# A four-stage vision block on one core: the weighting of a gathered row as one VectorE multiply or as four

## The chip, the cores and the metric

The kernel runs on one core of one Trainium2 chip. The metric is the device time of one execution in microseconds. Three runs of the kernel before took 13376.52, 13376.6 and 13379.08 us; the median is 13376.6 us.

## The reference

The input `x` is (4, 128, 128, 64) in float32. Four layers follow each other, each behind a residual or a normalisation: a 3x3 convolution with a 1x1 (L0), a deformable convolution (L1), a focal modulation with depthwise convolutions of 3, 5 and 7 taps (L2), and a triangle multiplication (L3). The change touches L1 alone. For each pixel, each of 2 channel groups and each of 9 taps, a position is worked out from learnt offsets, and 32 channels are sampled there bilinearly:

```python
out = wa[..., None] * gather(y0i, x0i) + wb[..., None] * gather(y1i, x0i) \
    + wc[..., None] * gather(y0i, x1i) + wd[..., None] * gather(y1i, x1i)
...
s = sampled.reshape(B, H, W, Kin)
s = _conv_same(s, dw_w[g], dw_b[g], groups=Kin)
s = _conv_same(s, pw_w[g], pw_b[g])
```

So 18 samples (2 groups by 9 taps) of four corners and 32 channels are wanted for every pixel.

## The kernel before

**The table.** Per image the kernel writes a table to device memory in which one entry holds the whole 2x2 patch of one group at one position: four corners of 32 channels, 128 floats (512 bytes). One indirect DMA, issued by GpSimd at L451, fetches one such entry for each of 128 pixels: an image row of 128 pixels lies across the 128 partitions, and `gat[r]` is [128, 18, 128]. A row of pixels thus takes 18 gathers. There are 4 images of 128 rows: 512 rows and 9216 gathers.

**The step.** Four rows (r = 0 to 3) make a step; each r has its own buffer `gat[r]`, its own indices `idx[:, r]` and its own semaphore `landed[r]`. GpSimd does nothing but this in the main part. Before the 18 gathers of row r it waits for `idx_given` (the indices of this row were copied) and for `summed` (the row that was in this buffer one step ago has been used up):

```python
pool.wait_ge(idx_given, v + 1)
pool.wait_ge(summed, v + 1)
```

**The row on VectorE.** `row()` waits for `landed[r]` and then issues, in this order: a copy of the next step's indices (`give_indices`, L1382), the multiply of all of `gat[r]` by the corner weights `wt` (L1406, 2304 elements per partition, both inputs in SBUF), a copy of the next weights (`give_weights`, L1385), the add of the right half of each entry to the left (L1411, 1152 elements, both inputs in SBUF), and the add of the two that remain into `srow` (L1418, 576 elements, both in SBUF). TensorE then turns `srow` (L1078, L1079), ScalarE copies it (L862, L863), and TensorE multiplies it with the folded depthwise and pointwise weights (L1085).

**What lies beside it.** `drive()` and `weave()` lay the stages of the other layers over the steps: while the gathers of image b run, VectorE, ScalarE and TensorE also work on the convolution, table and offsets of later images or on the modulation and triangle stages of the image before. Between two phases of `row()` (its `yield`s) their instructions stand on VectorE, as the `scalar_tensor_tensor` of L1291 and L1299, which read one input in PSUM, `bn_stats` at L1144, or the add at L1343 (`tt(res[u], lin[u], xt(...), ALU.add)`), which has both inputs in SBUF and 512 elements and is issued twice in a row. Before the first gather stands a prologue for image 0, and behind the last gather the remaining stages of image 3 run without any gather.

Of the kernel before, what the change touches and what calls it, by code (L numbers as in the profile page):

```python
# [25 lines left out]
ALU = mybir.AluOpType  # L26
# [5 lines left out]
P = 128  # L32
# [8 lines left out]
G, CG = 2, 32  # L41
GK = G * K9
# [128 lines left out]
def build(nc, x, mats, vecs, conv_kt, conv_w, off_w, dw_w, pw_w, dw_b, gate_w, base_loc, base_idx, taps,  # L171
          out):
    ctx = ExitStack()
    with ctx:
        def sb(name, shape, dt=F32):
            return ctx.enter_context(nc.sbuf_tensor(name, shape, dt))
# [4 lines left out]
        def sems(*names):  # L181
            return tuple(ctx.enter_context(nc.semaphore(n)) for n in names)
# [51 lines left out]
        wt = sb("wt", [P, ROWS, GK, 4])  # L234
# [61 lines left out]
        with nc.Block() as block:  # L296
# [64 lines left out]
        weighted, summed, turned, st_ready, rows_used, pair_done, pair_added, xr_in, x2_out = sems(  # L361
            "weighted", "summed", "turned", "st_ready", "rows_used", "pair_done", "pair_added", "xr_in", "x2_out")
# [68 lines left out]
        with nc.Block() as block:  # L431
# [705 lines left out]
            def _(dve):  # L1137
# [3 lines left out]
                stt_, tt, ts = nc.vector.scalar_tensor_tensor, nc.vector.tensor_tensor, nc.vector.tensor_scalar  # L1141
# [239 lines left out]
                def give_indices(v, r):  # L1381
                    nc.vector.tensor_copy(idx[:, r, :], idxn[:, r, :]).then_inc(idx_given, 1)  # L1382

                def give_weights(v, r):
                    nc.vector.tensor_copy(wt[:, r, :, :], wtn[:, r, :, :]).then_inc(wt_given, 1)  # L1385
# [10 lines left out]
                def row(n, r, give):  # L1396

                    v = n * ROWS + r
                    yield 3 * r
                    dve.wait_ge(landed[r], 16 * GK * (n + 1))  # L1400
                    if give:
                        give_indices(v, r)
                    dve.wait_ge(wt_given, v + 1)
                    g4 = gat[r][:].rearrange("p k (q c) -> p k q c", q=4)
                    wb = wt[:, r, :, :].unsqueeze(3).to_broadcast([P, GK, 4, CG])
                    tt(g4, g4, wb, ALU.mult).then_inc(weighted, 1)  # L1406
                    yield 3 * r + 1
                    dve.wait_ge(weighted, 2 * v + 1)
                    if give:
                        give_weights(v, r)  # L1410
                    tt(gat[r][:, :, 0:2 * CG], gat[r][:, :, 0:2 * CG], gat[r][:, :, 2 * CG:], ALU.add)\  # L1411
                        .then_inc(weighted, 1)
                    yield 3 * r + 2
                    dve.wait_ge(weighted, 2 * v + 2)
                    dve.wait_ge(turned, v + 1)
                    dst = srow[r % 2][:].rearrange("p (k g c) -> p g k c", g=G, c=CG)
                    src = gat[r][:].rearrange("p (g k) e -> p g k e", g=G)
                    tt(dst, src[:, :, :, 0:CG], src[:, :, :, CG:2 * CG], ALU.add).then_inc(summed, 1)  # L1418
# [12 lines left out]
                def step(n, b, i):  # L1431
                    last = isinstance(n, int) and n == STEPS - 1
                    yield 0
                    if isinstance(i, int) and i == PER - 1 and not last:
                        next_image(b + 1)
                    if not last:
                        indices(n + 1)
                    for r in range(ROWS):
                        yield from row(n, r, not last)
                        if r % 2 == 1:  # L1440
                            finish(n, r // 2)
                    if last:

                        dve.wait_ge(pair_done, 2 * STEPS + 1)
                        dve.wait_ge(x2_out, 16 * STEPS)
                        dve.wait_ge(xr_in, 16 * STEPS + 16)
                        stt_(xs[:, 0, :], acc[1][:, 0:W], b1, xr[:, 0, :], ALU.add, ALU.add).then_inc(pair_added, 1)
# [134 lines left out]
```

## Time and profile before

| | |
|---|---|
| median of three runs | 13376.6 us |
| profiled execution, first to last instruction | 13375.1 us |
| GpSimd (POOL) busy | 9661.0 us, 72% |
| TensorE matmul (PE) busy | 8114.2 us, 61% |
| VectorE (DVE) busy | 4255.4 us, 32% |
| ScalarE (ACT) busy | 1677.8 us, 13% |
| first gather starts, last gather starts | 242.7 us, 12686.7 us |

The time of the profiled execution is known by its span; it lies 1.5 us below the median of the runs. GpSimd's busy time counts the gathers' issue (the making of their descriptors), not the transfers, and the 0.30 us in front of each gather, in which its sequencer works for the next one, are not counted as busy. Busy shares are of the whole span, with the prologue and the end, in which GpSimd is idle.

### The profile page before, as it was taken

How to read it: one execution, taken by the hardware profiler on the slowest of the kernel's cores; microseconds unless marked ns; L12 is line 12 of the kernel's file. 1: busy time of each engine (PE TensorE's matmuls, PEld its weight loads, DVE VectorE, ACT ScalarE, POOL GpSimd, SP SyncE). 2: the span in 40 equal slices, each digit the busy share in tenths (PEclk: the TensorE clock that was granted, in tenths of full speed). 3: DMA queues.
4: the chain of work that ended last, by engine and by line, in shares of the span. 5: the costliest groups of instructions: out<-in, count | busy, mean ns of one | idle time of the engine just before them, and what ended most of it. 6: DMA issues, size and time to landing. Idle time of an engine off the chain costs nothing.

```text
span 13375.1 us, 136898 instructions
## 1 busy us (share of the span) xinstructions
PE 8114.2 (61%) x46082; PEld 6501.7 (49%) x46082; DVE 4255.4 (32%) x6850; ACT 1677.8 (13%) x3045; POOL 9661.0 (72%) x9269
## 2 busy tenths in 40 slices
PE   5666667666467765554457665654456675655487
PEld 3444445444456644444346654444446654444473
DVE  3233333333233332232233333232233333233233
ACT  1001101011010112110010011210000011210015
POOL 2777777777777777777777777777777777777700
PEclk7787778777678777776678777777678787777688
DMA  3333434334233422332233422332224422332164
GB/s 103 92 84 102 115 83 120 103 91 117 66 118 132 136 61 72 102 92 57 59 98 132 158 62 66 93 102 66 53 74 134 159 86 59 85 109 76 50 239 127
DMA packets 1033598, 1315.00 MB, mean 98 GB/s; under 512 B 186529, under 2 KB 831329, under 8 KB 1015969
## 3 DMA queue, kind: packets, MB, share of 16 engines
q0 software_dynamic: 294912, 604.57, 17.3%
q1 hardware_dynamic: 661664, 657.15, 15.0%
q10 hardware_dynamic: 76800, 50.34, 1.2%
q8 instruction: 138, 2.26, 0.1%
q14 instruction: 84, 0.68, 0.0%
HBM read 1082.07 MB, written 292.16 MB: 103 GB/s over the span
## 4 chain that ended last, share of the span: by engine, by line
POOL 71%; issue 22%; PE 3%; DMA 1%; DVE 1%; ACT 0%; SPq 0%; POOLq 0%; DVEq 0%; ACTq 0%; PEld 0%; PEldq 0%
POOL gat L451 71%; PE stage L982 2%; PE stage L885 1%; DMA table<-room 0%; PE acc L885 0%; DMA room<-b_d 0%; POOLq L449 0%; PE pt L885 0%; PE ptl L885 0%; PE stage L937 0%; POOLq L447 0%; POOLq L457 0%; DMA room<-x 0%; ACT room L776 0%; PE acc L1085 0%
## 5 line engine op out<-in xcount | busy, mean ns | idle before, releaser
L451 POOL DMA_INDIRECT gat<-table,idx x9216 | 9636.5, 1046 | 3010.1 <-issue 2804.4
L1085 PE MATMUL acc<-stt,wk 128*128 128x128 f32 (+1 forms) x30600 | 4502.0, 311 | 315.6 <-ACT stt L863 315.6
L1085 PEld LDWEIGHTS acc<-stt,wk 128*128 128x128 f32 (+1 forms) x30600 | 4259.1, 221 | 744.1 <-ACT stt L863 445.2
L1078 PE MATMUL pt<-mat,srow 128*128 128x128 f32 x2048 | 524.3, 405 | 3993.4 <-DVE srow L1418 3992.8
L1078 PEld LDWEIGHTS pt<-mat,srow 128*128 128x128 f32 x2048 | 342.4, 203 | 4193.4 <-DVE srow L1418 4167.2
L1382 DVE COPY idx<-idxn 128x18 uint32<-128x18 uint32 x512 | 98.1, 192 | 7115.7 <-DMA gat<-table,idx 7107.6
L885 PE MATMUL stage<-room,mat 128*128 128x512 f32 (+1 forms) x1696 | 1037.3, 745 | 574.2 <-DVE room L1291 124.4
L1406 DVE TENSOR_TENSOR gat<-gat,wt 128x2304 f32<-128x2304 f32 x512 | 1309.0, 2557 | 76.5 <-DMA gat<-table,idx 75.8
L862 ACT ACTIVATE stt<-pt 128x512 f32<-128x512 f32 x512 | 305.6, 597 | 7527.7 <-PE ptl L1079 7399.5
L982 PE MATMUL stage<-room 128*128 128x128 f32 x7680 | 892.4, 278 | 20.8 <-DMA room<-toep 18.7
L982 PEld LDWEIGHTS stage<-room 128*128 128x128 f32 x7680 | 877.2, 194 | 31.0 <-issue 22.3
L885 PEld LDWEIGHTS stage<-room,mat 128*128 128x128 f32 x1696 | 377.4, 247 | 1004.2 <-issue 468.3
L1411 DVE TENSOR_TENSOR gat<-gat 128x1152 f32<-128x1152 f32 x512 | 691.9, 1351 | 0.1
L1418 DVE TENSOR_TENSOR srow<-gat 128x576 f32<-128x576 f32 x512 | 388.5, 759 | 14.8
L937 PE MATMUL stage<-room,offw 128*72 (+1 forms) x768 | 369.6, 633 | 14.6 <-SPq L405 12.9
L913 PE MATMUL stage<-room,cw 128*128 (+1 forms) x768 | 347.4, 607 | 16.5 <-ACTq L405 14.3
L1361 DVE TENSOR_TENSOR loc<-off,base 128x144 f32<-128x144 f32 x128 | 39.3, 307 | 802.8 <-DMA off<-offs 802.8
L760 ACT ACTIVATE room<-stage 128x512 f32<-128x512 f32 x192 | 115.1, 599 | 1032.4 <-PE stage L982 1032.1
L913 PEld LDWEIGHTS stage<-room,cw 128*128 128x128 f32 x768 | 144.5, 193 | 189.9 <-issue 185.7
L937 PEld LDWEIGHTS stage<-room,offw 128*72 128x72 f32 x768 | 112.6, 154 | 222.9 <-issue 209.7
L1079 PE MATMUL ptl<-mat,srow 128*64 128x128 f32 x512 | 201.1, 393 | 0.0
L691 ACT ACTIVATE room<-room,gn 128x512 f32 x256 | 192.3, 805 | 37.6 <-PEq L405 35.9
(180 smaller groups left out, 4031.3 us busy)
## 6 DMA issues: line engine op xcount, KB each, us to landing
gat<-table,idx POOLq DMA_INDIRECT x9216
room<-toep SPq DMA_DIRECT2D x64, 1792.0 KB, 18.4
room<-toep SPq DMA_DIRECT2D x64, 1280.0 KB, 11.3
table<-room SPq DMA_DIRECT2D x128, 512.0 KB
room<-toep SPq DMA_DIRECT2D x64, 768.0 KB, 5.0
toep<-in_taps SPq DMA_DIRECT2D x128, 224.0 KB
toep<-in_taps SPq DMA_DIRECT2D x128, 160.0 KB
room<-in_x SPq DMA_DIRECT2D x4, 4096.0 KB, 15.2
```

The source lines that it names most:

```text
L451: nc.gpsimd.indirect_dma_start(gat[r][:, k, :], None, table[b][0:NENT * ENTRY].rearrange("(n e) -> n e", e=ENTRY), bass.IndirectOffsetOnAx ...
L862: nc.scalar.activation(stt[r % 2][:, 0:4, 1:W + 1], pt[:], ACT.Copy)
L885: return nc.tensor.matmul(dst, w, r, start=True, stop=True)
L913: ins = nc.tensor.matmul(PB[u][:], cw0[:, 2 * k:2 * k + 2, :].rearrange("p a c -> p (a c)"), window(k // 3, k % 3, t), start=(k == 0), sto ...
L937: ins = nc.tensor.matmul(PB[0][0:2 * NOFF, :], offw[:, k, :], window(k // 3, k % 3, 2 * i + u), start=(k == 0), stop=(k == 5))
L982: ins = nc.tensor.matmul(PB[2 * u + l % 2][:, c * W:(c + 1) * W], band[l][u][:, c * k + dx, :], cin[l][u][:, c, at:at + W], start=(dx == 0 ...
L1078: nc.tensor.transpose(pt[:, m, :], srow[r % 2][:, m * P:(m + 1) * P], M["ident"])
L1079: nc.tensor.transpose(ptl[:, r % 2, :], srow[r % 2][:, 4 * P:KC], M["ident"]).then_inc(turned, 1)
L1085: ins = nc.tensor.matmul(acc[a][:, 0:W], wk[0:kk, m, dx, block_at * C:block_at * C + P], stt[s][0:kk, m, dx:dx + W], start=start and m == ...
L1406: tt(g4, g4, wb, ALU.mult).then_inc(weighted, 1)
L1411: tt(gat[r][:, :, 0:2 * CG], gat[r][:, :, 0:2 * CG], gat[r][:, :, 2 * CG:], ALU.add)\
L1418: tt(dst, src[:, :, :, 0:CG], src[:, :, :, CG:2 * CG], ALU.add).then_inc(summed, 1)
```

## The change

In `row()` the one multiply becomes four, one for each corner q of the 2x2 patch. Each multiplies the 32 channels of that corner in all 18 entries (18 x 32 = 576 elements per partition, in chunks of 32 with a step of 128) by the weight of that corner. They work in place on separate parts of `gat[r]`; the first waits for `wt_given` as the one multiply did, and none of the others waits for anything. All four count up `weighted`, so the two waits behind them count in fives.

```diff
@@ -1402,16 +1402,17 @@
                         give_indices(v, r)
                     dve.wait_ge(wt_given, v + 1)
                     g4 = gat[r][:].rearrange("p k (q c) -> p k q c", q=4)
-                    wb = wt[:, r, :, :].unsqueeze(3).to_broadcast([P, GK, 4, CG])
-                    tt(g4, g4, wb, ALU.mult).then_inc(weighted, 1)
+                    for q in range(4):
+                        wb = wt[:, r, :, q:q + 1].to_broadcast([P, GK, CG])
+                        tt(g4[:, :, q, :], g4[:, :, q, :], wb, ALU.mult).then_inc(weighted, 1)
                     yield 3 * r + 1
-                    dve.wait_ge(weighted, 2 * v + 1)
+                    dve.wait_ge(weighted, 5 * v + 4)
                     if give:
                         give_weights(v, r)
                     tt(gat[r][:, :, 0:2 * CG], gat[r][:, :, 0:2 * CG], gat[r][:, :, 2 * CG:], ALU.add)\
                         .then_inc(weighted, 1)
                     yield 3 * r + 2
-                    dve.wait_ge(weighted, 2 * v + 2)
+                    dve.wait_ge(weighted, 5 * v + 5)
                     dve.wait_ge(turned, v + 1)
                     dst = srow[r % 2][:].rearrange("p (k g c) -> p g k c", g=G, c=CG)
                     src = gat[r][:].rearrange("p (g k) e -> p g k e", g=G)
```

On VectorE the row r = 1 of the first step reads so in the program before (the words in brackets are the semaphores that an instruction waits for):

```order
L1382 COPY idx<-idxn 128x18 [waits landed1]
L1406 TENSOR_TENSOR gat<-gat,wt 128x2304 [waits wt_given]
L1385 COPY wt<-wtn 128x72 [waits weighted]
L1411 TENSOR_TENSOR gat<-gat 128x18x64
L1418 TENSOR_TENSOR srow<-gat 128x2x9x32 [waits turned,weighted]
```

and so in the changed one, where the lines behind the multiply have moved on by one:

```order
L1382 COPY idx<-idxn 128x18 [waits landed1]
L1407 TENSOR_TENSOR gat<-gat,wt 128x18x32 [waits wt_given]
L1407 TENSOR_TENSOR gat<-gat,wt 128x18x32 x3
L1385 COPY wt<-wtn 128x72 [waits weighted]
L1412 TENSOR_TENSOR gat<-gat 128x18x64
L1419 TENSOR_TENSOR srow<-gat 128x2x9x32 [waits turned,weighted]
```

Nothing else moves: the three other multiplies stand directly behind the first, and no instruction of another stage comes between them. The other engines' programs are the same.

## Rows read from the trace of the kernel before

**Rows 1.** The page: busy time and shares, and the busy tenths in 40 slices.
```profile
PE 8114.2 (61%) x46082; PEld 6501.7 (49%) x46082; DVE 4255.4 (32%) x6850; ACT 1677.8 (13%) x3045; POOL 9661.0 (72%) x9269
...
DVE  3233333333233332232233333232233333233233
...
POOL 2777777777777777777777777777777777777700
```

**Rows 2.** The page: the chain of waits that ended last, by engine and line.
```profile
POOL 71%; issue 22%; PE 3%; DMA 1%; DVE 1%; ACT 0%; SPq 0%; POOLq 0%; DVEq 0%; ACTq 0%; PEld 0%; PEldq 0%
```

**Rows 3.** Costliest groups: busy, mean ns of one | idle just before, what ended it.
```profile
L451 POOL DMA_INDIRECT gat<-table,idx x9216 | 9636.5, 1046 | 3010.1 <-issue 2804.4
...
L1382 DVE COPY idx<-idxn 128x18 uint32<-128x18 uint32 x512 | 98.1, 192 | 7115.7 <-DMA gat<-table,idx 7107.6
```

**Rows 4.** The gather's line: ns min/median/max, first and last start, its waits.
```profile
L451 POOL DMA_INDIRECT gat<-table,idx x9216: 940/944/3314, 242.7 to 12686.7; - x197
...
  issue: 2804.4, 9202
  DVE idx L1382: 202.1, 2
  DVE srow L1418: 3.7, 12
```

**Rows 5.** Timeline: start us, us, engine line op, [idle before <-releaser]; one row of pixels.
```profile
5020.16 0.94 POOL L451 DMA_INDIRECT gat<-table,idx  x1 [0.30 <-issue]
5021.41 0.94 POOL L451 DMA_INDIRECT gat<-table,idx  x1 [0.30 <-issue]
5021.52 0.18 DVE L1382 COPY idx<-idxn 128x18 uint32<-128x18 uint32 x1 [16.67 <-DMA gat<-table,idx]
5021.61 2.56 DVE L1406 TENSOR_TENSOR gat<-gat,wt 128x2304 f32<-128x2304 f32 x1
5022.66 2.33 POOL L451 DMA_INDIRECT gat<-table,idx  x1 [0.30 <-issue]
5024.09 1.40 DVE L1291 SCALAR_TENSOR_TENSOR room<-stage,vec,room 128x512 f32<-128x512 f32 x2
...
5025.29 0.94 POOL L451 DMA_INDIRECT gat<-table,idx  x1 [0.30 <-issue]
...
5025.51 1.35 DVE L1411 TENSOR_TENSOR gat<-gat 128x1152 f32<-128x1152 f32 x1
...
5026.54 1.14 POOL L451 DMA_INDIRECT gat<-table,idx  x1 [0.30 <-issue]
...
5026.90 0.76 DVE L1418 TENSOR_TENSOR srow<-gat 128x576 f32<-128x576 f32 x1
```

**Rows 6.** Timeline: the multiply of the next step, met earlier by a gather.
```profile
5053.65 2.55 DVE L1406 TENSOR_TENSOR gat<-gat,wt 128x2304 f32<-128x2304 f32 x1
5054.19 2.82 POOL L451 DMA_INDIRECT gat<-table,idx  x1 [0.31 <-issue]
...
5056.42 1.35 DVE L1411 TENSOR_TENSOR gat<-gat 128x1152 f32<-128x1152 f32 x1
5057.32 1.27 POOL L451 DMA_INDIRECT gat<-table,idx  x1 [0.30 <-issue]
```

**Rows 7.** Timeline: a gather that starts inside a VectorE instruction with no second SBUF tensor.
```profile
5002.00 0.69 DVE L1144 BATCH_NORM_STATS2 stats<-room  x1
5002.07 0.94 POOL L451 DMA_INDIRECT gat<-table,idx  x1 [0.30 <-issue]
```

**Rows 8.** Lines L1343, L1406, L1411 and L1418: ns min/median/max of one, first and last start.
```profile
L1343 DVE TENSOR_TENSOR room<-room x64: 679/684/691, 5753.8 to 13371.4; 128x512 f32<-128x512 f32 x64
...
L1406 DVE TENSOR_TENSOR gat<-gat,wt x512: 2544/2558/2615, 267.0 to 12689.2; 128x2304 f32<-128x2304 f32 x171
L1411 DVE TENSOR_TENSOR gat<-gat x512: 1335/1352/1358, 269.7 to 12691.8; 128x1152 f32<-128x1152 f32 x171
L1418 DVE TENSOR_TENSOR srow<-gat x512: 690/758/805, 271.1 to 12693.2; 128x576 f32<-128x576 f32 x171
```

**Rows 9.** Timeline: a gather beside the two adds of L1343, issued one behind the other.
```profile
5902.38 1.29 DVE L1343 TENSOR_TENSOR room<-room 128x512 f32<-128x512 f32 x2
5902.45 1.43 POOL L451 DMA_INDIRECT gat<-table,idx  x1 [0.30 <-issue]
```

## The prediction

> **What bounds the kernel now.** I read the busy shares first: GpSimd is at 8 tenths in every slice from the second until the gathers end, and VectorE never over 4 tenths [rows 1]. The chain of waits says the same: 71% GpSimd and 22% "issue", the 0.30 us before each gather [rows 2]. What counts is the cost of a gather. The groups and the gather's own line give a median of 944 ns, a mean of 1046 and a longest of 3314 [rows 3, 4]. Undisturbed, a gather comes every 0.944 + 0.305 = 1.25 us (2804.4 us over 9202 gaps), a row of 18 every 22.5 us. The 9216 gathers run from 242.7 to 12686.7 us, which is 24.3 us per row. The missing 1.8 us per row is the gap between mean and median: 102 ns x 9216 = 940 us. GpSimd hardly ever waits on a semaphore: 3.7 us in all for L1418, and 202.1 us for the first indices [rows 4].
>
> The timeline tells where the 940 us sit. The multiply of L1406 runs from 5021.61 to 5024.17. The gather of 5022.66 takes 2.33 us and ends at 5024.99, 0.82 us after the multiply's end. In the next step the multiply ends at 5056.20 and the gather at 5057.01: 0.81 us after, though it began at another moment of the multiply [rows 5, 6]. The adds of L1411 do the same: ends at 5026.86 and 5057.77, gathers done at 5027.68 and 5058.59, each 0.82 us later. So a gather needs something about 0.944 - 0.82 = 0.12 us after its start that it gets only when the VectorE instruction is over. I call this moment its **read**. A gather that starts 0.07 us into a `bn_stats` takes its plain 0.94 us [rows 7], so it is not VectorE's being busy as such. The instructions that hold it here have two inputs in SBUF, and a gather has its indices there.
>
> The Trainium skill (SBUF — State Buffer, § Who interferes with whom) says that a VectorE instruction with two SBUF inputs contends with a GpSimd instruction that reads SBUF, and that the loser of this lock blocks for the whole instruction; the trace agrees, with the 0.82 us behind the end each time.
>
> **What the change does to one row.**
>
> *The four parts.* Each has 576 elements. No such multiply is in the trace; the nearest row is L1418, 576 elements in chunks of 32 from SBUF, 758 ns median, 690 to 805 [rows 8]. The line through 1152 elements (1352 ns) and 2304 (2558) gives 1.047 ns per element and 146 ns fixed, so 749 ns; I take 0.75. Without a wait between them instructions overlap: the two adds of L1343 take 0.684 us each and 1.29 us together [rows 8, 9], so the second starts 0.60 us after the first, 0.08 us before its end. Four parts thus start 0.67 us apart and end 0.75, 1.42, 2.09 and 2.76 us after the start. The multiply as a whole gets longer by 0.20 us.
>
> *Who gets in between the parts.* This decides the sign. [Rows 9] is the case: two overlapping adds with two SBUF inputs each, and a gather that starts at 5902.45, 0.07 us after the first. It took 1.43 us and ended at 5903.88. The first add ended at 5902.38 + 0.68 = 5903.06, and 0.82 us later is 5903.88; the second ended at 5903.67, which would have given 5904.49. So the waiting gather passes at the seam, even with no gap between the instructions.
>
> *The row.* In [rows 5] the read comes at 5022.78, 1.17 us into the multiply. Before, it is let go at 2.56 us. Now it falls in part 2, is let go at 1.42, and the next read follows 1.25 us later at 2.67, in part 4, and is let go at 2.76. Everything behind (the copy, the add, the next read 1.25 us on) then stands as before, 0.20 us later, with one more gather done. The gain is 1.25 - 0.20 = **1.05 us per row**. In [rows 6] the read comes at 0.66 us. Before: let go at 2.56, the next at 3.81, held by the add until 4.12. Now: let go at 0.75, then 2.00 (held to 2.09), then 3.34, held by the add until 4.32. Again one gather more and 0.20 us lost: 1.05 us. The add brings both cases back into step, so I take 1.05 for all rows.
>
> *The sum.* 511 rows (the last multiply starts at 12689.2, behind the last gather [rows 8, 4]) x 1.05 us = 537 us. With parts at L1418's own median of 758 ns the multiply would be 0.03 us longer and the sum 521 us; I take 534, nearer to the fitted line. The check from above: all that the multiplies can cost is the 940 us less the adds' share (0.20 and 0.33 us in the two rows read, some 135 us), so 800 us, and 534 leaves some held time, as it must.
>
> *What is free.* VectorE works 0.20 us more per row, 102 us in all, and one more instruction's issue three times. It is idle 7107.6 us waiting for gathers to land before L1382 [rows 3]. The add of the row in [rows 5] ends at 5027.66; its buffer is wanted again three rows after 5020.16, at 5093, so there are 65 us of slack where 0.20 us are used. With rows of 23.3 us the slack shrinks by 3 us. The later release of `srow` falls on a TensorE that is only 61% busy [rows 1]. The counts of `weighted` in fives cost some register work on VectorE's queue, under the same cover. If this cover were gone, the 102 us would be paid. The prologue (243 us) and the end behind the last gather (13375.1 - 12687.6 = 688 us) hold no row but the last and stay.
>
> 13375.1 - 534 = 12841 us against the profiled span; the median of the runs lies 1.5 us above it, so **12843 us**.
>
> **The rivals.**
>
> *A: the four parts hold the gather as one.* The next part takes the inputs before the waiting gather does, and the read is let go at 2.76 instead of 2.56. Every row then costs 0.20 us more: 13377 + 102 = **13479 us**, slower. It decides as soon as GpSimd loses the seam. For it: the parts overlap by 0.08 us, and VectorE's next instruction is already issued. Against it: [rows 9], a seam of the same kind that the gather won; but such seams are few in this trace. 7%.
>
> *B: no overlap, or gaps.* With 0.04 us between the parts they end at 0.75, 1.54, 2.33 and 3.12. The multiply is 0.56 us longer, one gather more still passes, and the gain is 1.25 - 0.56 = 0.69 us, 353 us in all: **13024 us**. Against it: the 1.29 us of two adds in [rows 9]. 12%. The Trainium skill (VectorE: DVE Perf Modes, § The DRAIN you can't avoid) says that the next operation does not start until the pipeline is empty; by that the parts would end 0.75 us apart, the last at 3.00, and the gain would be 0.81 us per row, 414 us, giving 12963 us. The rows show an overlap instead.
>
> *C: nothing.* The multiply is not what holds the gather, or the total time of holding is what counts, and it is the same split or whole. **13377 us.** For it: nothing but that VectorE works at least as long as before. Against it: four gathers in [rows 5, 6], let go at four ends. 3%. The Trainium skill (SBUF — State Buffer, § Who interferes with whom) infers that `tensor_tensor` does not stall the making of descriptors for a DMA that GpSimd issues; by that a split would bring nothing. This trace speaks against it.
>
> *D: shorter parts.* At L1418's 690 ns the parts end at 0.69, 1.30, 1.91 and 2.52: the second read of [rows 5] comes at 2.55 and is free, the row gains 1.26 us, 644 us in all: **12733 us**. 8%, since 690 is that line's fastest, not its median.
>
> **How the numbers follow.** The forecast, parts of 0.74 to 0.76 us that overlap and let the gather pass, has 70%. The range goes from D, 12730, to B, 13030; A and C lie outside it with 10%. A measurement of this kernel tells 0.2% (27 us) from no change. Faster: forecast, B and D, 0.90. Same: C, 0.03. Slower: A, 0.07.
>
> **What would show it.** If right: the mean of the gather's line falls from 1046 to 1046 - 534000/9216 = 988 ns with its median at 944 and 0.30 us still before each; the longest gathers, 2.3 to 2.8 us beside the multiply, are gone and turn into some of 1.0 to 1.7 us that end 0.82 us behind a part's end; four multiplies of 0.75 us start 0.67 us apart; VectorE's busy time grows, since its records overlap, by 4 x 0.75 - 2.56 = 0.44 us a row, 225 us; its wait before L1382 shrinks by some 600 us. Rival A would show gathers that end 0.82 us behind the fourth part. B would show the parts 0.79 us apart. A wait of GpSimd on L1419 of more than a few us would mean that the slack was not there. The prediction is wrong if the seam is lost, or if the parts are much longer than L1418.

## The result, and the profile after

The changed kernel took 12838.01 us (median of four runs, 12835.18 to 12846.34) where the kernel before took 13376.99 us beside it (13376.52 to 13379.08): a ratio of 0.9599, 95% interval 0.9585 to 0.9612. It is 539 us faster; 12843 us was forecast.

The page of the kernel after: its span, busy times, GpSimd's busy tenths, and the costliest groups.

```profile
span 12839.0 us, 138434 instructions
...
PE 8043.8 (63%) x46082; PEld 6435.5 (50%) x46082; DVE 4362.9 (34%) x8386; ACT 1679.1 (13%) x3045; POOL 9123.5 (71%) x9269
...
POOL 2777777777777777777777777777777777777600
...
POOL 68%; issue 23%; PE 4%; DVE 2%; DMA 1%; ACT 0%; SPq 0%; POOLq 0%; DVEq 0%; ACTq 0%; PEld 0%; PEldq 0%
...
L451 POOL DMA_INDIRECT gat<-table,idx x9216 | 9099.0, 987 | 3009.7 <-issue 2774.6
...
L1382 DVE COPY idx<-idxn 128x18 uint32<-128x18 uint32 x512 | 96.4, 188 | 6489.7 <-DMA gat<-table,idx 6481.7
...
L1407 DVE TENSOR_TENSOR gat<-gat,wt 128x576 f32<-128x576 f32 x2048 | 1415.0, 752 | 71.4 <-DMA gat<-table,idx 71.0
```

Against [rows 1 to 3]: the mean gather is 987 ns instead of 1046, GpSimd's time in them fell by 9636.5 - 9099.0 = 537.5 us, and the span by 13375.1 - 12839.0 = 536.1 us. The chain is still GpSimd's. The gain is all in L451. TensorE and ScalarE do nearly what they did (8043.8 us against 8114.2, and 1679.1 against 1677.8).

The gather's line after: durations, and what GpSimd waited for.

```profile
L451 POOL DMA_INDIRECT gat<-table,idx x9216: 940/944/2497, 241.9 to 12148.4; - x197
...
  issue: 2774.6, 9104
  DVE idx L1382: 201.9, 3
  DVE srow L1419: 33.2, 109
```

The median stands at 944 ns as in [rows 4]; it is the tail of long gathers that went. The 33.2 us for L1419 look like a new wait and are none: 33.2 us in 109 times is the 0.30 us in front of every gather, in which VectorE happened to finish its add, and 2774.6 + 33.2 = 2807.8 us stand against the 2804.4 + 3.7 = 2808.1 us of [rows 4].

The timeline of one row after, as [rows 5] before (start us, us, engine, line, operation):

```profile
5001.05 0.94 POOL L451 DMA_INDIRECT gat<-table,idx  x1 [0.30 <-issue]
5001.18 2.75 DVE L1407 TENSOR_TENSOR gat<-gat,wt 128x576 f32<-128x576 f32 x4
5002.30 1.11 POOL L451 DMA_INDIRECT gat<-table,idx  x1 [0.30 <-issue]
5003.71 1.03 POOL L451 DMA_INDIRECT gat<-table,idx  x1 [0.30 <-issue]
5004.08 1.35 DVE L1412 TENSOR_TENSOR gat<-gat 128x1152 f32<-128x1152 f32 x1
5005.05 1.19 POOL L451 DMA_INDIRECT gat<-table,idx  x1 [0.30 <-issue]
```

Four parts of 0.75 us take 2.75 us together, so they start 0.67 us apart and end 0.75, 1.42, 2.08 and 2.75 us after 5001.18. The read of the gather of 5002.30 comes 1.24 us in, in part 2. The gather ends at 5003.41, 0.81 us behind that part's end. The next read (5003.83) is in part 4, and its gather ends at 5004.74, 0.81 us behind the end of the run at 5003.93. The third is held by the add as before. Where one gather passed by the multiply's end, two do now.

One row could be chance, so I counted all gathers of both traces, taking the read 0.127 us after a gather's start. Before, 511 gathers are held by the multiply, for 728.6 us in all beyond their plain 0.944 us, and the adds of L1411 hold 511 more for 150.4 us. After, the four parts hold 1008 gathers, nearly two a row, for 158.6 us, and the adds of L1412 again 511, for 182.0 us. Of the gathers after, 549 have their read in a part that another one follows at once, 0.16 us or more behind its start and before its last 0.02 us. All 549 end 0.81 to 0.84 us behind the end of their own part; not one is held on by the next.

### The profile page after: what moved, and what is told of

Same layout as the page of the kernel before. It is cut to its first block, busy times and chain, and to the rows that moved or that the text cites. A ratio compares the mean times of both kernels' runs of the same rounds, so it can differ in the third digit from the quotient of the medians.

```text
span 12839.0 us, 138434 instructions
## 1 busy us (share of the span) xinstructions
PE 8043.8 (63%) x46082; PEld 6435.5 (50%) x46082; DVE 4362.9 (34%) x8386; ACT 1679.1 (13%) x3045; POOL 9123.5 (71%) x9269
## 4 chain that ended last, share of the span: by engine, by line
POOL 68%; issue 23%; PE 4%; DVE 2%; DMA 1%; ACT 0%; SPq 0%; POOLq 0%; DVEq 0%; ACTq 0%; PEld 0%; PEldq 0%
POOL gat L451 68%; PE stage L982 2%; PE stage L885 1%; DMA gat<-table,idx 1%; DVE gat L1407 1%; DMA table<-room 0%; PE acc L885 0%; DMA room<-b_d 0%; DVE gat L1412 0%; DVE srow L1419 0%; DVE room L1299 0%; POOLq L449 0%; PE pt L885 0%; PE ptl L885 0%; DVE room L1203 0%
## 5 line engine op out<-in xcount | busy, mean ns | idle before, releaser
L451 POOL DMA_INDIRECT gat<-table,idx x9216 | 9099.0, 987 | 3009.7 <-issue 2774.6
L1085 PE MATMUL acc<-stt,wk 128*128 128x128 f32 (+1 forms) x30600 | 4442.0, 308 | 315.8 <-ACT stt L863 315.8
L1085 PEld LDWEIGHTS acc<-stt,wk 128*128 128x128 f32 (+1 forms) x30600 | 4199.3, 218 | 742.3 <-ACT stt L863 443.0
L1382 DVE COPY idx<-idxn 128x18 uint32<-128x18 uint32 x512 | 96.4, 188 | 6489.7 <-DMA gat<-table,idx 6481.7
L1407 DVE TENSOR_TENSOR gat<-gat,wt 128x576 f32<-128x576 f32 x2048 | 1415.0, 752 | 71.4 <-DMA gat<-table,idx 71.0
L885 PE MATMUL stage<-room,mat 128*128 128x512 f32 (+1 forms) x1696 | 1036.7, 744 | 492.6 <-DVE room L1291 110.8
L1412 DVE TENSOR_TENSOR gat<-gat 128x1152 f32<-128x1152 f32 x512 | 691.7, 1351 | 0.1
L1419 DVE TENSOR_TENSOR srow<-gat 128x576 f32<-128x576 f32 x512 | 388.4, 759 | 14.8
```

Source lines behind the costliest of these rows:

```text
L451: nc.gpsimd.indirect_dma_start(gat[r][:, k, :], None, table[b][0:NENT * ENTRY].rearrange("(n e) -> n e", e=ENTRY), bass.IndirectOffsetOnAx ...
L885: return nc.tensor.matmul(dst, w, r, start=True, stop=True)
L1085: ins = nc.tensor.matmul(acc[a][:, 0:W], wk[0:kk, m, dx, block_at * C:block_at * C + P], stt[s][0:kk, m, dx:dx + W], start=start and m == ...
L1407: tt(g4[:, :, q, :], g4[:, :, q, :], wb, ALU.mult).then_inc(weighted, 1)
```

## Experiments

I call **theory S** what the prediction rests on: a gather's read waits for the end of the VectorE instruction with two inputs in SBUF that it falls into, and passes at the seam. What a cut is worth then depends on how many reads pass before the row's work is over. **Rival M** says that shorter parts are better, whatever their seams. **Rival F** says that the form of the access was what mattered.

The numbers expected were counted by moving the reads of the trace before over the altered VectorE instructions, with 146 ns + 1.047 ns per element for each, 0.08 us of overlap, a hold that begins 0.14 us after a start, and a read 0.127 us after the gather's.

### Two parts, three parts, nine parts

The edit, with N = 2, 3 or 9 (and the waits on `weighted` counted to match):

```diff
-                    tt(g4, g4, wb, ALU.mult).then_inc(weighted, 1)
+                    for k in range(0, GK, GK // N):
+                        tt(g4[:, k:k + GK // N], g4[:, k:k + GK // N], wb[:, k:k + GK // N], ALU.mult)\
+                            .then_inc(weighted, 1)
```

Two parts:

> The one multiply is cut in two along the 18 entries, 9 entries (1152 elements) each, instead of in four by corner. Theory S (a read waits for the end of the two-input instruction that it falls into and passes at the seam): parts of 1.35 us that start 1.27 us apart end 1.35 and 2.62 us after the start. The usual read at 1.17 passes at 1.35, the next at 2.60 falls into the last 0.02 us and passes at 2.62; one more gather per row for 0.06 us more multiply: 1.19 us per row, 608 us, with the reads of the rows at other moments counted 600 us: 12776 us. Rival M (what counts is the mean time left of a part, so shorter parts are always better): about two reads per row that each wait half a part, 1.35 us in all against 1.43 us held now: hardly a gain, 13250 to 13350 us. Rival F (the gain comes from the form, chunks of 32 with a step of 128, and not from the cut): 13377 us.

**12770.49 us** (12769.5 to 12771.58), ratio to the kernel before 0.9551 (0.9535 to 0.9567). Its timeline:

```profile
5043.76 2.63 DVE L1407 TENSOR_TENSOR gat<-gat,wt 128x1152 f32<-128x1152 f32 x2
5044.84 1.09 POOL L451 DMA_INDIRECT gat<-table,idx  x1 [0.30 <-issue]
5046.24 0.96 POOL L451 DMA_INDIRECT gat<-table,idx  x1 [0.30 <-issue]
5046.53 1.35 DVE L1413 TENSOR_TENSOR gat<-gat 128x1152 f32<-128x1152 f32 x1
```

The first gather ends at 5045.93, 0.82 us behind the first part's end (5043.76 + 1.35). The second read, at 5046.37, comes 0.02 us before the second part's end at 5046.39 and waits those 0.02 us. Two long parts beat four short ones by 68 us (the ratios to the kernel before, 0.9551 and 0.9599, lie apart by more than their intervals).

Three parts:

> The multiply is cut in three along the 18 entries, 6 entries (768 elements, 0.95 us) each. Theory S: ends at 0.95, 1.82 and 2.69 us; the usual read at 1.17 passes only at 1.82, the next comes at 3.07, behind the multiply, and falls into the add (2.83 to 4.18). So no further gather gets through before the add's end, and the add ends 0.13 us later than before: these rows gain nothing, and only those whose read comes early gain a gather. Counted over the reads of the trace: 107 us less, 13270 us; far worse than two parts or four. Rival M: between two parts and four, and better than two: 13000 to 13200 us. Rival F: 13377 us.

**13266.53 us** (13265.42 to 13278.8), ratio 0.9925 (0.9908 to 0.9941). Its timeline:

```profile
5020.20 2.68 DVE L1407 TENSOR_TENSOR gat<-gat,wt 128x768 f32<-128x768 f32 x3
5021.33 1.50 POOL L451 DMA_INDIRECT gat<-table,idx  x1 [0.30 <-issue]
5023.03 1.35 DVE L1413 TENSOR_TENSOR gat<-gat 128x1152 f32<-128x1152 f32 x1
5023.13 2.06 POOL L451 DMA_INDIRECT gat<-table,idx  x1 [0.30 <-issue]
```

The read at 5021.46 falls into the second part and waits for its end, 1.82 us in. The next, at 5023.26, misses the gap between the multiply (ends at 5022.88) and the add and is held by the whole add, 2.06 us for one gather. By the add's end no gather more has passed than before, and the cut is worth almost nothing. Neither M nor F can give this: three parts lie neither between two and four nor at 13377.

Nine parts:

> The multiply is cut in nine along the 18 entries, 2 entries (256 elements, 0.41 us) each. Theory S: the parts start 0.33 us apart and the multiply ends at 3.09 us, 0.53 us later than whole; one more gather per row, and part of it given back: counted over the reads of the trace 445 us less, 12932 us, slower than four parts by 90 us. Rival M: nine parts are better than four, 12750 to 12830 us. Rival F: 13377 us.

**12935.76 us** (12934.38 to 12938.34), ratio 0.9674 (0.9658 to 0.969). The multiply's group:

```profile
L1407 DVE TENSOR_TENSOR gat<-gat,wt 128x256 f32<-128x256 f32 x4608 | 1592.8, 418 | 71.2 <-DMA gat<-table,idx 70.8
```

1592.8 us over 512 rows are 3.11 us per row against 2.76 with four parts: each further part adds its fixed time. Counted as above, the parts hold the gathers for 129.9 us in all instead of 158.6, but the add behind the longer multiply now holds them for 311.3 us instead of 182.0. Rival M wanted this to be the best cut.

### The changed kernel with waits between its parts

```diff
                         tt(g4[:, :, q, :], g4[:, :, q, :], wb, ALU.mult).then_inc(weighted, 1)
+                        if q < 3:
+                            dve.wait_ge(weighted, 5 * v + q + 1)
```

> The changed kernel, but each of the second, third and fourth multiply waits for the one before it, so that they no longer overlap. Theory S, as rival B of the prediction: parts end at 0.75, 1.54, 2.33 and 3.12 us, 355 us less than the kernel before: 13022 us, 184 us more than the changed kernel. Had GpSimd's read passed in the changed kernel only because some gap was left between the parts, a wider gap would cost nothing or help: 12800 to 12860 us. A rival by which the overlap is not there even now: no difference, 12838 us.

**13018.85 us** (13013.44 to 13025.03), ratio 0.9737 (0.972 to 0.9753). One row of it:

```profile
5002.54 3.13 DVE L1407 TENSOR_TENSOR gat<-gat,wt 128x576 f32<-128x576 f32 x4
5003.02 1.09 POOL L451 DMA_INDIRECT gat<-table,idx  x1 [0.30 <-issue]
5004.42 1.28 POOL L451 DMA_INDIRECT gat<-table,idx  x1 [0.30 <-issue]
```

The four take 3.13 us instead of 2.75. The gathers end at 5004.11 and 5005.70, 0.82 and 0.81 us behind the ends of parts 1 and 3 (0.75 and 2.34 us in). So a gather passes at a seam with a gap of 0.04 us as it does where the parts overlap by 0.08. The gap isn't needed, and it isn't free: the multiply that is 0.38 us longer costs 181 us of the 539.

### One instruction more, with one input or with two

Both kernels put one instruction of 2304 elements more between the two adds of each row of the changed kernel, and count `weighted` in sixes:

```diff
+                    nc.vector.tensor_reduce(rsc[:], gat[r][:], AX.X, ALU.add).then_inc(weighted, 1)
+                    dve.wait_ge(weighted, 6 * v + 6)
...
+                    tt(gat[r][:], gat[r][:], gat[r][:], ALU.max).then_inc(weighted, 1)
+                    dve.wait_ge(weighted, 6 * v + 6)
```

The second changes no value (the maximum of a number with itself), the first writes to a tile that nobody reads.

> Once more, since on the two chips that took this kernel until now the kernel before itself took 17.6 and 17.8 ms. The changed kernel with one VectorE instruction more in each row between its two adds, the maximum of gat with itself in place (2304 elements, both inputs in SBUF, 2.56 us, values unchanged), as long as the multiply was. Theory S: it holds a gather's read until it ends; counted over the reads of the trace 693 us more than the changed kernel, 13531 us, where the kernel before takes some 13375 us. If two inputs in SBUF did not matter, it would be hidden: 12838 us.

**13537.19 us** (13532.67 to 13542.04), where the kernel before took 13375.26; ratio 1.0123 (1.0106 to 1.014).

> Once more, since on the two chips that took this kernel until now the kernel before itself took 17.6 and 17.8 ms. The changed kernel with one VectorE instruction more in each row between its two adds, a sum over each of the 18 entries of gat (2304 elements, one input in SBUF, 2.55 us, its result unused). Theory S: it does not hold a gather, and VectorE has some 60 us of slack per row: no change from the changed kernel, 12838 us within 15 us, although VectorE works 1.3 ms longer in all and as long as with the two inputs, which took 13537 us. If any VectorE work of this length did it: 13537 us too.

**12829.96 us** (12823.9 to 12833.24), where the kernel before took 13372.79; ratio 0.9593 (0.9577 to 0.9609), the changed kernel's own. The two instructions are of the same length, as the groups and one row of each show; first the kernel with two inputs:

```profile
L451 POOL DMA_INDIRECT gat<-table,idx x9216 | 9787.6, 1062 | 3009.6 <-issue 2755.9
...
L1416 DVE TENSOR_TENSOR gat<-gat 128x2304 f32<-128x2304 f32 x512 | 1310.0, 2559 | 14.8
...
5008.03 2.56 DVE L1416 TENSOR_TENSOR gat<-gat 128x2304 f32<-128x2304 f32 x1
5009.12 2.29 POOL L451 DMA_INDIRECT gat<-table,idx  x1 [0.30 <-issue]
```

and then the kernel with one:

```profile
DVE idx L1383: 5177.5, 433
...
L452 POOL DMA_INDIRECT gat<-table,idx x9216 | 9091.2, 986 | 3009.5 <-issue 2776.2
...
L1417 DVE TENSOR_REDUCE rsc<-gat 128x18 f32<-128x2304 f32 x512 | 1305.6, 2550 | 14.8
...
5031.14 2.55 DVE L1417 TENSOR_REDUCE rsc<-gat 128x18 f32<-128x2304 f32 x1
5032.23 0.94 POOL L452 DMA_INDIRECT gat<-table,idx  x1 [0.30 <-issue]
```

In the same place of the row, 1.09 us into the instruction, the gather takes 2.29 us beside two inputs and 0.94 beside one. Over the whole trace 511 gathers are held by the instruction with two inputs, for 696.9 us in all, and of the 981 whose read falls well inside the one with a single input (over 0.14 us in, over 0.06 us before its end) none is. 1.3 ms of VectorE work cost 699 us in one form and nothing in the other. It also shows that VectorE's slack is real: its wait for gathers only shrank, from 6481.7 to 5177.5 us.

The two kernels differ in more than the inputs: the sum is another operation, and it writes 18 elements where the maximum writes 2304. The trace of the kernel before has cases that tell these apart. L1295 is the same `tensor_tensor` with one of its inputs in PSUM, and L1211 a `memset` that writes 2304 elements to SBUF and reads none:

```profile
4934.69 1.29 DVE L1295 TENSOR_TENSOR room<-stage,room 128x512 f32<-128x512 f32 x2 [4.20 <-ACT room L780]
4935.56 0.94 POOL L451 DMA_INDIRECT gat<-table,idx  x1 [0.30 <-issue]
...
1051.09 1.98 DVE L1211 MEMSET room<- 128x2304 f32 x1 [0.43 <-DVE gat L1406]
1051.78 0.94 POOL L451 DMA_INDIRECT gat<-table,idx  x1 [0.30 <-issue]
```

In that trace 10 reads fall well inside an L1295, 6 inside an L1211, and 24 inside an L1291, which has two inputs, one of them in PSUM, and writes 512 elements. All 40 gathers take at most 0.95 us. So it is neither the operation nor the writing that holds a gather, but the second input in SBUF.

### The halves with the add cut as well, and two chips on which no expected time was met

```diff
-                    tt(gat[r][:, :, 0:2 * CG], gat[r][:, :, 0:2 * CG], gat[r][:, :, 2 * CG:], ALU.add)\
-                        .then_inc(weighted, 1)
+                    for k in (slice(0, 14), slice(14, GK)):
+                        tt(gat[r][:, k, 0:2 * CG], gat[r][:, k, 0:2 * CG], gat[r][:, k, 2 * CG:], ALU.add)\
+                            .then_inc(weighted, 1)
```

This kernel and the two of the section above also ran on two other chips, and there the kernel before itself took 17585.03 and 17806.04 us. What was expected on the first of these chips, for the halves with the cut add, one input more and two inputs more:

> The multiply in two parts of 9 entries, and the first add of the row (L1411) in two of 14 and 4 entries (896 and 256 elements, 1.08 and 0.41 us, 1.00 us apart). Theory S: with the multiply in halves the reads come at 1.35, 2.62 and 3.87 us; the add's first part runs from about 2.76 to 3.84 and is over when the third read comes, or nearly so, so that most of the add's hold falls away: counted over the reads 716 us less than the kernel before, 12661 us, 115 us less than the halves alone. It stands on 0.05 us, so if the reads come 0.1 us earlier or later than I take them it gives 12750 to 12800 us. Rival M: 13100 us.

> The changed kernel with one VectorE instruction more in each row between its two adds, a sum over each of the 18 entries of gat (2304 elements, one input in SBUF, about 2.5 us, its result unused). Theory S: an instruction with one SBUF input does not hold the gather, and VectorE has some 60 us of slack per row: no change from the changed kernel, 12838 us within 15 us, although VectorE works 1.2 ms longer in all. A rival by which VectorE's being busy, or its lateness, is what the gathers feel: 512 x 1 to 2.5 us more, 13350 to 14100 us.

> The changed kernel with one VectorE instruction more in each row between its two adds, the maximum of gat with itself in place (2304 elements, both inputs in SBUF, about 2.56 us, values unchanged). It is as long as the multiply was. Theory S: it holds a gather's read until it ends; counted over the reads of the trace 693 us more than the changed kernel, 13531 us, with gathers in it that end 0.82 us behind its end. If the number of inputs does not matter, this kernel and the one with one input more take the same time.

They took 17935.01 us (ratio 1.0209), 18186.25 us (1.0341) and 17384.51 us (0.9877). On the second chip:

> The multiply in two parts of 9 entries, and the first add of the row (L1411) in two of 14 and 4 entries (896 and 256 elements, 1.08 and 0.41 us, 1.00 us apart). Theory S: with the multiply in halves the reads come at 1.35, 2.62 and 3.87 us; the add's first part runs from about 2.76 to 3.84 and is over when the third read comes, or nearly so, so that most of the add's hold falls away: counted over the reads 716 us less than the kernel before, 12661 us, 115 us less than the halves alone. It stands on 0.05 us, so if the reads come 0.1 us earlier or later than I take them it gives 12750 to 12800 us. Rival M (shorter parts are always better): more than the 12770 us of the halves can't be had from the multiply, and the add's cut gives half a part, 0.2 us a row: 12670 us too; it does not tell the two apart and stands here as a version that may beat both kernels.

> The changed kernel with one VectorE instruction more in each row between its two adds, a sum over each of the 18 entries of gat (2304 elements, one input in SBUF, 2.55 us, its result unused). Theory S: an instruction with one SBUF input does not hold the gather, and VectorE has some 60 us of slack per row: no change from the changed kernel, 12838 us within 15 us, although VectorE works 1.3 ms longer in all. A rival by which VectorE's being busy, or its lateness, is what the gathers feel: 512 x 1 to 2.5 us more, 13350 to 14100 us.

> The changed kernel with one VectorE instruction more in each row between its two adds, the maximum of gat with itself in place (2304 elements, both inputs in SBUF, 2.56 us, values unchanged). It is as long as the multiply was. Theory S: it holds a gather's read until it ends; counted over the reads of the trace 693 us more than the changed kernel, 13531 us. If the number of inputs does not matter, this kernel and the one with one input more take the same time.

They took 18218.29 us (1.0231), 18420.55 us (1.0344) and 17535.96 us (0.9857): no number expected was met, and the order of the three is the same both times. The results of the section above are from chips on which the kernel before took some 13375 us. The halves with the cut add did not run on such a chip, so its 12661 us are untested.

What was different there can be read in part. TensorE's waits in the kernel with one input more, on the second of these chips:

```profile
PE acc L1086 <- issue: 3147.2, 1632, 69.8
PE acc L1086 <- ACT stt L864: 2135.9, 323, 74.1
```

TensorE stood for 3.1 ms in front of the products (up to 69.8 us at once) with nothing in the profile that it waited for, while GpSimd was down to 49% busy (72% in the kernel before at 13375.1 us, where TensorE's products had no such wait and 315.6 us for ScalarE's copy). The profile puts 21% of the chain that ended last down to "another core or an unknown queue". With GpSimd no longer the pace, shortening its waits can't be expected to pay. What held TensorE up is open. The times say nothing on theory S. The gathers in these traces still follow it: on the second chip 308 gathers are held by the instruction with two inputs and end 0.81 to 0.83 us behind it, and none of the 482 whose read falls well inside the one with a single input is held.

## Why the prediction was right

**The bound.** GpSimd's gathers were the pace and still are; 536.1 us of span answer to 537.5 us of gather time. It is so for every cut: against the kernel before, the pages of two, three and nine parts and of four with waits show 607.2, 110.8, 438.5 and 355.6 us less in the gathers, and 607.4, 110.8, 438.6 and 356.9 us less span.

**The seam.** The sign hung on [rows 9], one pair of overlapping adds. That was thin evidence for the step that decided the sign, and the prediction gave rival A 7%. The trace after bears it out: all 549 gathers that could have been held on by a following part went at the seam, so rival A is out.

**The row.** "One gather more, and the multiply 0.20 us longer": measured 2.75 or 2.76 us against 2.56, and 539 / 511 = 1.05 us per row, as forecast. It is made up as the prediction had it: the multiply holds gathers for 570.0 us less in all, 1.12 us a row, and the add, which comes later, for 31.6 us more. "1.05 for all rows" was taken from two rows read; the sum bears it out, and rows at other moments were not worked out in it. That the add brings the reads back into step is what the thirds show from the other side: there it swallows the gather that the multiply let go late.

**The other cuts** were expected from the same account, and none was missed by more than 9 us: 12776, 13270, 12932, 13022, 13531 and 12838 us were expected, 12770, 13267, 12936, 13019, 13537 and 12830 measured (two, three and nine parts, waits, two inputs and one input more).

**Rival B** was priced at 13024 us; with its condition made, the kernel takes 13018.85. **Rival C** is out by the counts: with much the same time under the multiply in a row (2.63, 2.75 and 2.68 us for two, four and three parts) the kernel takes 12770, 12838 or 13267 us by where the seams are. **Rival D** did not come about: the parts are 752 ns on average, as the line through the longer ones gave, and not 690.

The Trainium skill (SBUF — State Buffer, § Who interferes with whom) has both sides of this. Its rule that two SBUF inputs contend with a GpSimd instruction that reads SBUF agrees with the pair of one and two inputs (12830 and 13537 us). Its inference that `tensor_tensor` does not stall a DMA issued from GpSimd doesn't hold for these indirect ones. Under rival B the prediction cites one sentence of VectorE: DVE Perf Modes, § The DRAIN you can't avoid, by which the parts would not overlap. The same paragraph of the Trainium skill goes on that a next operation that isn't held back by the earlier ones starts earlier, and the starts 0.67 us apart for parts of 0.75 us agree with that.

**What was off.** VectorE's busy time was to grow by 225 us and grew by 107.5 (4255.4 to 4362.9): I added the four durations, but the page counts the overlap once, and 1415.0 us over 512 rows are 2.76 us. The prediction's own 0.20 us a row, 102 us in all, was the right figure. Its check put everything but the adds' share down to the multiplies, some 800 us; counted, the multiplies held gathers for 728.6 us, and some 58 us belong to other stages. I also wrote that a wait of GpSimd on L1419 of more than a few us would speak against the slack; 33.2 us stand there, and they are the ordinary 0.30 us under another name.

**What is open.** That the read fetches the gather's indices is inferred from when it happens and from what holds it; no run here moved the indices. Shown is only that a gather waits at that moment, and for what. Weights in PSUM, which would leave the whole multiply one SBUF input, were not tried: all eight banks are written by TensorE while the gathers run. The best measured version is the multiply in halves, 12770 us.

## What to carry to other kernels

Where gathers issued by GpSimd set the pace, look at the gap between their mean and median duration, and at what ends a fixed time before the long ones do: a VectorE instruction may cost nothing on VectorE and a microsecond on GpSimd. Whether to cut it is decided by where the seams lie against the gathers' rhythm (1.25 us here): two parts gave 4.5%, three 0.75%, four 4.0%. Draw the row out on paper before cutting; shorter is not better by itself.

## What the runs showed of the hardware that was not expected

An instruction with two SBUF inputs does not hold from its very start. In the kernel with two parts:

```profile
5004.36 2.67 DVE L1407 TENSOR_TENSOR gat<-gat,wt 128x1152 f32<-128x1152 f32 x2
5004.37 0.94 POOL L451 DMA_INDIRECT gat<-table,idx  x1 [0.30 <-issue]
```

The gather starts 0.01 us after the multiply, its read comes 0.13 us in, and it runs its plain 0.94 us. If a part behind another begins to hold as late, an overlap of 0.08 us leaves a free moment of about 0.05 us at a seam, which would be why the waiting gather gets in.

The changed kernel's trace lets this be checked, if the read is again taken 0.127 us after a gather's start. At the seams of the multiply 13 reads fall 0.087 to 0.153 us behind the start of a later part, and all 13 gathers run plain. Where the read comes 0.161 us in or later and over 0.05 us before the part's end, every gather is held to that end. With the part before it over 0.08 us in, the free moment at these seams is some 0.07 us long. Its length isn't the same everywhere: reads 0.094 us into the add of L1412 are held. That a gather which already waits gets in by this moment fits, but isn't shown by it.

And not every seam lets a gather through. The longest gather that is left in the changed kernel stands beside a run of `tensor_scalar`, which have one SBUF tensor and their scalars in SBUF:

```profile
1556.78 5.95 DVE L1181 TENSOR_SCALAR room<-room,gn  x12
...
1560.35 2.50 POOL L451 DMA_INDIRECT gat<-table,idx  x1 [0.30 <-issue]
```

The run ends at 1562.73 and the gather at 1562.85, 0.12 us behind it rather than 0.82: it is held just before its own end, and past three seams of the run that come after 1561.29, where its plain 0.944 us would have ended. Two gathers before it in the same run, at 1557.61 and 1558.96, got away at seams: they take 1.05 and 1.09 us and end 0.12 us behind the end of an instruction inside the run. All six runs of this kind under the gathers show the same, 2.49 to 2.50 us for the last gather. So it is a second way of holding, at another moment of the gather, and why one seam lets a gather go and another does not is open. The stage with L1181 is short, so it costs little here (under 16 us in all); what a cut would do to it was not tried.
